# Denominators of a cross-attention through DRAM instead of through a selector product

## What is computed

```
q = shape(query_states @ wq, T);  k = shape(key_value_states @ wk, S);  v = shape(key_value_states @ wv, S)
scores = jnp.einsum('bhtd,bhsd->bhts', q, k) + bias
weights = jax.nn.softmax(scores, axis=-1)
attn = jnp.einsum('bhts,bhsd->bhtd', weights, v)
return transpose(attn) @ wo
x = layernorm(x + cross_attention)
```

## Time and profile before

| | us |
|---|---|
| median of 3 runs | 1098.14 |
| lowest, highest | 1097.65, 1098.8 |
| the profiled execution | 1090.97 |
| its span in the trace | 1089.2 |
| of it: up to the first batch's scores | 154 |
| the 32 batches' scores and what lies between | 154 to 924 |
| projection and feed-forward net | from 932.8 |

### The profile page before, as it was taken

How to read it: one execution, slowest core, us unless ns; L and a number is a source line. 1 busy time by engine, 2 the same in 40 slices (tenths; PEclk the granted TensorE clock), 3 DMA queues, 4 the chain that set the end, 5 groups by cost and what they waited for, 6 DMA issues and landing times. The chain is left out here.

```text
span 1089.2 us, 25588 instructions
## 1 busy us (share of the span) xinstructions
PE 962.5 (88%) x10410; PEld 654.0 (60%) x10410; DVE 717.2 (66%) x1521; ACT 599.0 (55%) x1059; POOL 401.7 (37%) x409
## 2 busy tenths in 40 slices
PE   6474289999999999999999999999999998799996
PEld 4263056666666666666666666666666666545564
DVE  3447277878878777878878777878877874540014
ACT  2132036666666666666666667666666766352232
POOL 7034004555554444555554444555554400000000
PEclk9757579999999999999999999999999999899999
DMA  8664814565556656665555666656555430300000
GB/s 248 163 198 116 170 63 148 171 190 178 164 177 179 191 170 210 181 185 178 163 178 179 191 192 188 186 179 178 164 177 174 141 92 3 109 0 1 1 9 25
DMA packets 57198, 158.16 MB, mean 145 GB/s; under 512 B 23906, under 2 KB 35322, under 8 KB 54010
## 3 DMA queue, kind: packets, MB, share of 16 engines
q1 hardware_dynamic: 57082, 156.54, 48.6%
HBM read 112.40 MB, written 42.63 MB: 142 GB/s over the span
## 5 line engine op out<-in xcount | busy, mean ns | idle before, releaser
L107 DVE TENSOR_REDUCE cmax<-max_ps 112x1 f32<-112x512 f32 x512 | 337.2, 683 | 150.8 <-PE max_ps L97 150.8
L765 ACT ACTIVATE e_sb<-st_ps 128x896 f32<-128x896 f32 (+1 forms) x384 | 354.1, 925 | 149.5 <-DVE st_ps L710 90.4
L97 PE MATMUL max_ps<-kst,qst 111*112 111x512 bf16 x760 | 283.6, 401 | 35.6 <-PEq L116 13.3
L609 PEld LDWEIGHTS st_ps<-qst,kst 114*128 114x128 bf16 (+1 forms) x3072 | 190.6, 101 | 82.0 <-issue 41.9
L811 POOL TENSOR_TENSOR kpart<-k_left,kpart 128x500 bf16<-128x500 f32 x87 | 99.3, 1141 | 344.6 <-ACT k_left L782 340.1
L609 PE MATMUL st_ps<-qst,kst 114*128 114x112 bf16 (+1 forms) x3072 | 214.7, 213 | 12.4 <-DMA qst<-nmp 11.2
L104 DVE CUSTOM_DVE_ANT_0 near_out<-max_ps,near_nat 112x476 bf16<-112x476 f32 x248 | 154.1, 649 | 23.8 <-PE max_ps L97 23.7
L97 PEld LDWEIGHTS max_ps<-kst,qst 111*112 111x112 bf16 x760 | 92.3, 129 | 102.5 <-DVE cmax L107 39.2
L637 PE MATMUL pv_ps<-e_sb,vals 128*32 128x168 f32 (+1 forms) x3072 | 149.4, 312 | 0.3 <-ACT e_sb L765 0.3
L681 PE MATMUL misc<-wv,ctxt 128*128 128x128 f32 (+1 forms) x768 | 107.4, 284 | 6.5 <-DMA ctxt<-in_ctxT 6.5
L681 PEld LDWEIGHTS misc<-wv,ctxt 128*128 128x128 f32 (+1 forms) x768 | 99.5, 193 | 22.3 <-ACT vals L750 11.5
(11 more groups left out here) (124 smaller groups left out, 923.4 us busy)
## 6 DMA issues: line engine op xcount, KB each, us to landing
kst<-kparts SPq DMA_DIRECT2D x192, 375.0 KB, 6.2
kparts<-kpart SPq DMA_DIRECT2D x96, 375.0 KB, 2.7
ctxt<-in_ctxT SPq DMA_DIRECT2D x32, 750.0 KB, 7.1
qst<-qslots SPq DMA_DIRECT2D x192, 28.0 KB, 6.1
qslots<-qst SPq DMA_DIRECT2D x1, 2688.0 KB, 14.5
vals<-in_ctxT SPq DMA_DIRECT2D x3, 750.0 KB, 13.3
h<-in_h SPq DMA_DIRECT2D x2, 1024.0 KB, 7.7
qst<-nmp SPq DMA_DIRECT2D x96, 1.8 KB
```

The costliest lines, as they stand in the source:

```text
L97: return nc.tensor.matmul(dst[0:TT, 0:hi - lo], m.qst[0:M_ROW, r, p, :], m.kst[0:M_ROW, r, p, lo:hi], start=True, stop=True)
L107: return nc.vector.tensor_reduce(m.cmax[:, r, c, p:p + 1], src[0:TT, 0:BOUND[c + 1] - BOUND[c]], AX.X, ALU.max)
L609: mm = nc.tensor.matmul(st_ps[0:K, j % 2, p // 4, (p % 4) * TT:(p % 4 + 1) * TT], m.kst[0:AUG, u % RING, p, j * P:j * P + K], m.qst[0:AUG, ...
L765: nc.scalar.activation(e_sb[0:K, j % E_RING, :].rearrange("p (a c) -> p a c", a=2), st_ps[0:K, j % 2, :, 0:HALF], ACT.Exp).then_inc(s_ex, 1)
```

## The change

The denominators no longer pass through TensorE. Once `x_sb` is there, SyncE stores the four rows of sums into a DRAM buffer `dens` (two DMAs, the second one twice as wide by a broadcast), waits until they are stored, and loads them back spread over the rows (five DMAs) into `den`, as three pieces of 56 columns: one for the twelve heads' groups, two to be added. These stand in SyncE's list between the query pieces and the store of key part 0, with the context load between stores and loads. GpSimd masks `x_sb` itself, adds the pieces (two operations), waits for the loads and adds the two pieces of denominators, all between third 0 and third 1 of the keys. VectorE takes one reciprocal of 112 columns in slot 7 and one product into `m.xh` in slot 9. `sel`, its two products and the copy to `den` are gone.

```
@@ MISC
-        MISC = {0: ("v", 0, 1), 1: ("v", 1, 1), 2: ("v", 2, 1), 3: ("den", 0, -1),
-                4: ("k", 0, 3), 5: ("k", 1, 3), 6: ("k", 2, 3), M0: ("nmt", 0, 1)}
-        NM, REC_A, REC_B, XH = M0 - 1, 4, 5, 9
+        MISC = {0: ("v", 0, 1), 1: ("v", 1, 1), 2: ("v", 2, 1), 4: ("k", 0, 3), 5: ("k", 1, 3), 6: ("k", 2, 3), M0: ("nmt", 0, 1)}
+        NM, REC, XH = M0 - 1, 7, 9
@@ TensorE
-                    if kind == "den":
-                        pe.wait_ge(s_xr, n + 1)
-                        nc.tensor.matmul(misc[:, 0:A_COLS], sel[:, 0, :], x_sb[:, 0:A_COLS], start=True, stop=True)
-                        nc.tensor.matmul(misc[:, A_COLS:A_COLS + B_COLS], sel[:, 1, :],
-                                         x_sb[:, A_COLS:A_COLS + B_COLS], start=True, stop=True).then_inc(s_dn, 1)
@@ VectorE
-                    if j == XH and live(g, u - 1):
-                        dve.wait_ge(s_ro, b)
-                        nc.vector.tensor_tensor(x_own[:, :], x_sb[:, :], rec[:, :], ALU.mult).then_inc(s_xo, 1)
...
-                        if j == REC_A:
-                            dve.wait_ge(s_dr, b)
-                            nc.vector.reciprocal(rec[:, 0:A_COLS], den[:, 0:A_COLS]).then_inc(s_rc, 1)
-                        if j == REC_B:
-                            nc.vector.reciprocal(rec[:, A_COLS:A_COLS + B_COLS],
-                                                 den[:, A_COLS:A_COLS + B_COLS]).then_inc(s_rc, 1)
+                        if j == REC:
+                            dve.wait_ge(s_db, b)
+                            nc.vector.reciprocal(rec[:, :, :], den[:, 0:2, :]).then_inc(s_rc, 1)
                         if j == XH:
-                            dve.wait_ge(s_xo, b)
-                            for i, (lo, hi) in enumerate(((0, A_COLS), (A_COLS, A_COLS + B_COLS))):
-                                nc.vector.tensor_reduce(m.xh[:, i, bass.ds((b - 1) * T, T)],
-                                                        x_own[:, lo:hi].rearrange("p (i t) -> p t i", t=T),
-                                                        AX.X, ALU.add).then_inc(s_xh, 1)
+                            dve.wait_ge(s_rc, b)
+                            dve.wait_ge(s_xs, 2 * b)
+                            nc.vector.tensor_tensor(m.xh[:, :, (b - 1) * T:b * T], x_sum[:, :, :], rec[:, :, :],
+                                                    ALU.mult).then_inc(s_xh, 1)
@@ ScalarE
                         wait(act, s_xo, b - 1)
+                        wait(act, s_ds, 32 * (b - 1))
                         nc.scalar.copy(x_sb[:, :], pv_ps[:, 0:PIECES * T]).then_inc(s_xr, 1)
...
-                        if kind == "den":
-                            act.wait_ge(s_dn, n + 1)
-                            nc.scalar.copy(den[:, :], misc[:, 0:PIECES * T]).then_inc(s_dr, 1)
@@ GpSimd, between split_k(g, u, 0) and split_k(g, u, 1)
-                    pool.wait_ge(s_rc, 2 * b)
-                    nc.gpsimd.tensor_tensor(rec[:, :].rearrange("p (i t) -> p i t", t=T),
-                                            rec[:, :].rearrange("p (i t) -> p i t", t=T),
+                    pool.wait_ge(s_xr, b)
+                    nc.gpsimd.tensor_tensor(x_own[:, :, :], x_sb[:, :].rearrange("p (i t) -> p i t", t=T),
                                             own[:, :].unsqueeze(2).broadcast_to([P, PIECES, T]),
-                                            ALU.mult).then_inc(s_ro, 1)
-                    pool.wait_ge(s_ro, b)
+                                            ALU.mult).then_inc(s_xo, 1)
+                    pool.wait_ge(s_xo, b)
+                    wait(pool, s_xh, b - 1)
+                    nc.gpsimd.tensor_tensor(x_sum[:, :, :], x_own[:, 0:4:3, :], x_own[:, 1:5:3, :],
+                                            ALU.add).then_inc(s_xs, 1)
+                    pool.wait_ge(s_xs, 2 * b - 1)
+                    nc.gpsimd.tensor_tensor(x_sum[:, 0, :], x_sum[:, 0, :], x_own[:, 2, :],
+                                            ALU.add).then_inc(s_xs, 1)
+                    pool.wait_ge(s_dl, 80 * b)
+                    nc.gpsimd.tensor_tensor(den[:, 1, :], den[:, 1, :], den[:, 2, :], ALU.add).then_inc(s_db, 1)
+                    pool.wait_ge(s_db, b)
@@ SyncE, behind stack_k and stack_q
+                if live(g, u - 1):
+                    sp.wait_ge(s_xr, b)
+                    wait(sp, s_dl, 80 * (b - 1))
+                    totals = x_sb[31:P:32, :]
+                    sp.dma_start(m.dens[0, :, :], totals[:, 0:A_COLS + T]).then_inc(s_ds, 16)
+                    sp.dma_start(m.dens[1, :, :].rearrange("q (a c) -> q a c", a=2),
+                                 totals[:, A_COLS:A_COLS + B_COLS].unsqueeze(1).broadcast_to([4, 2, B_COLS])
+                                 ).then_inc(s_ds, 16)
                 if live(g, u + 4):
                     if live(g, u + 1):
                         sp.wait_ge(s_vp, 3 * (b + 2))
                     load_ctx(b + 4, u + 4)
+                if live(g, u - 1):
+                    sp.wait_ge(s_ds, 32 * b)
+                    wait(sp, s_xh, b - 1)
+                    rows = m.dens[0, :, :].rearrange("q (k t) -> (q k) t", t=T).unsqueeze(1)
+                    sp.dma_start(den[:, 0, :], rows.broadcast_to([16, 8, T])).then_inc(s_dl, 16)
+                    for h in range(2):
+                        for i in range(2):
+                            rows = m.dens[1, 2 * i:2 * i + 2, :].rearrange("q (k t) -> (q k) t", t=T).unsqueeze(1)
+                            sp.dma_start(den[64 * h:64 * h + 64, 1 + i, :],
+                                         rows.broadcast_to([8, 8, T])).then_inc(s_dl, 16)
                 if later(g, u + 3):
                     sp.wait_ge(s_kf, 3 * (b + 1))
                     store_k(u + 3, 0)
```

More of the change, by code:

```diff
@@ L500, in cross_attention_block @@
         wk, wv = sb("wk", [C, C]), sb("wv", [C, C])
-        sel = sb("sel", [P, 2, P])
         ctxt = sb("ctxt", [C, RING, S])
@@ L508, in cross_attention_block @@
         nmp, nm_left = sb("nmp", [PAIRS, 3, TT], BF16), sb("nm_left", [PAIRS, TT])
-        x_sb, den, rec = sb("x_sb", [P, PIECES * T]), sb("den", [P, PIECES * T]), sb("rec", [P, PIECES * T])
-        own, x_own = sb("own", [P, PIECES]), sb("x_own", [P, PIECES * T])
+        x_sb, x_own, own = sb("x_sb", [P, PIECES * T]), sb("x_own", [P, PIECES, T]), sb("own", [P, PIECES])
+        x_sum, den, rec = sb("x_sum", [P, 2, T]), sb("den", [P, 3, T]), sb("rec", [P, 2, T])
         max_ps = ctx.enter_context(nc.psum_tensor("max_ps", [P, 2, 512], F32))
@@ L521, in cross_attention_block @@
         s_mx, s_mr = m.s_mx, m.s_mr
-        s_st, s_kp, s_vp, s_nt, s_pv, s_dn = (sem(n) for n in ("st", "kp", "vp", "nt", "pv", "dn"))
-        s_kf, s_ve, s_ex, s_xr, s_nr, s_dr = (sem(n) for n in ("kf", "ve", "ex", "xr", "nr", "dr"))
-        s_kr, s_k3, s_np, s_ro = sem("kr"), sem("k3"), sem("np"), sem("ro")
+        s_st, s_kp, s_vp, s_nt, s_pv = (sem(n) for n in ("st", "kp", "vp", "nt", "pv"))
+        s_kf, s_ve, s_ex, s_xr, s_nr = (sem(n) for n in ("kf", "ve", "ex", "xr", "nr"))
+        s_kr, s_k3, s_np = sem("kr"), sem("k3"), sem("np")
+        s_ds, s_dl, s_xs, s_db = sem("ds"), sem("dl"), sem("xs"), sem("db")
         s_nb, s_nm, s_rc, s_xo, s_xh = (sem(n) for n in ("nb", "nm", "rc", "xo", "xh"))
@@ L596, in misc_free @@
                     else:
-                        pe.wait_ge(s_dr if kind == "den" else s_nr, n + 1)
+                        pe.wait_ge(s_nr, n + 1)
                     return
@@ L669, in iteration @@
                     if isinstance(g, int) and u == -1:
-                        pe.wait_ge(s_w, 16 * 4)
+                        pe.wait_ge(s_w, 16 * 2)
                     misc_free(pe, g, u, j)
@@ L884, in _ @@
                 sp.dma_start(dst[:, :], src).then_inc(s_w, 16)
-            for i in range(2):
-                sp.dma_start(sel[:, i, :], d["sel"][i]).then_inc(s_w, 16)
             for n in range(RING):
@@ L893, in _ @@
             run(iteration)(sp)
-            sp.wait_ge(s_xh, 2 * B)
+            sp.wait_ge(s_xh, B)
 def ffn_block(nc, d, m):
@@ L1124, in build @@
             "(r i c s) -> r i c s", r=RING, i=3, c=C)
+        m.dens = nc.dram_tensor("dens", (2, 4, A_COLS + T), F32, kind="Internal").ap()
         m.s_qd = [ctx.enter_context(nc.semaphore(f"qd{g}")) for g in range(NG)]
```

## The result

| | before | changed |
|---|---|---|
| median of 4 runs, us | 1097.89 | 1238.72 |
| lowest, highest | 1091.1, 1098.8 | 1234.11, 1243.13 |
| profiled execution | 1090.97 | 1239.88 |

The ratio is 1.132, 95% interval 1.128 to 1.135. Keys' loads are 29.47 us apart where they were 24.63.

A forecast was written before the change was run, and what follows sets the result against it. TensorE looked like the bound, each batch closed by GpSimd's chain to `nmp` that just outlasts it. 131 + 6.5 - 1.6 + 4.6 = +140.5 us on the profiled 1091.0, plus 7.1 for the median: 1238 us, range 1165 to 1290.

The forecast's parts named there:

- 28 periods: Batches that load keys: the period grows from 24.63 to 29.3 us, 4.7 us more for 28 batches, +131 us.
- 29th batch: Batch that loads keys but splits none: TensorE is through 24.6 us after the keys' load instead of 18.1, +6.5 us.
- last two batches: Batches with an empty DMA queue: each gains 0.8 us, -1.6 us together.
- `x_sb` to `xh` at the end: End chain with copy, stores, loads, sum, reciprocal and product: 10.1 us instead of 5.5, +4.6 us.
- The loop: Keys' load, stores, denominator loads, third 1, `nmp`, third 2, last key store, next keys' load: 29.3 us, without TensorE.
- rival 1: SyncE's queue: small transfers pass large ones, stores land 2.4 us after issue; period 27.2, +79 us, 1177 us; chance 0.14.
- The mis-sized term: From GpSimd's third 1 to the next keys' load: kept at its old distance of 11.57 us.
- TensorE's fit: TensorE inside the 29.3 us period: stalls near 4 us mid-batch and 1.4 at the end, isn't the bound.
- rival 3: TensorE halts some 4 us a batch and its clock falls; 1 us a batch beyond the stalls, 1266 us; chance 0.08.
- A wait counted twice: TensorE before its first score product waits for `nmp` into `qst`: 20.1 + 11.2 = 31.3 us, 1.0 a batch.
- rival 2: Denominators come in time, only GpSimd's longer list counts: +1.5 - 0.8 = 0.7 a batch, +20 us, 1118 us; chance 0.05.
- rival 4: TensorE's own 95% sets the batch, GpSimd operations and DMAs find room: faster, 1077 us; chance 0.05.

The follow-up runs named there:

- all_late: The changed kernel with GpSimd's four operations behind third 2 and VectorE's reciprocal and product in slots 4 and 5 of the next iteration: 1086.0 us, ratio 0.990.
- pool_ops: The kernel before with three small GpSimd sums (112, 56, 56 columns) into an unread tile behind the mask: 1135.1 us, ratio 1.035.
- late_rec7: all_late with VectorE's reciprocal and product back in slots 7 and 9: 1301.7 us, ratio 1.187.
- act_stores: The changed kernel with the two stores issued by ScalarE on its own queue, right behind its copy to `x_sb`: 1176.8 us, ratio 1.071.

## Why the prediction was right, point by point

| term | predicted, us | measured, us |
|---|---|---|
| 28 periods | +131 | (1008.23 - 183.04) - 689.64 = +135.5 |
| first keys' load, 183.04 for 181.75 | 0 | +1.3 |
| 29th batch, 24.8 for 18.1 | +6.5 | +6.7 |
| last two batches | -1.6 | -1.6 |
| `x_sb` to `xh` at the end, 9.0 for 5.5 | +4.6 | +3.5 |
| projection and feed-forward, 161.7 for 158.2 | 0 | +3.5 |
| sum | 140.5 | 148.9 |

The measured terms are read from these rows: first and last keys' load, the scores after it, and the end chain.

```profile
183.04 0.53 SPq L82 DMA_DIRECT2D kst<-kparts  x1
...
1008.23 1.16 SPq L82 DMA_DIRECT2D kst<-kparts  x2
...
1033.06 0.56 PE L608 MATMUL st_ps<-qst,kst 114*128 114x112 bf16 x8
```

```profile
1068.79 0.39 ACT L758 COPY x_sb<-pv_ps 128x280 f32<-128x280 f32 x1 [1.09 <-PE pv_ps L645]
...
1076.24 0.30 POOL L821 TENSOR_TENSOR den<-den 128x56 f32<-128x56 f32 x1 [5.38 <-DMA den<-dens]
...
1077.47 0.28 DVE L720 TENSOR_TENSOR xh<-x_sum,rec 128x112 f32<-128x112 f32 x1
1078.21 8.99 PE L974 MATMUL ff_ps<-wo_sb,xh 128*112 128x128 f32 x64 [9.49 <-PEq L497]
```

**The median is nearer than the sum deserves.** The terms came out 8.4 us short. What made up for it is the 7.1 us added from the profiled execution of before to its median: in the changed kernel the median lies 1.2 us below the profiled execution. Within the range, but luck.

**The loop, step by step.** The mechanism was as forecast, and its main link was placed well. From keys' load to the first load of `den` it is 12.68 us in the mean; 12.4 was forecast, 10.2 by rival 1. The stores complete 4.7 us after the second's issue, and behind an empty queue in the last batches 1.6 to 1.7: that rejects rival 1. In the trace the completion semaphore of the two stores is raised twice right after their issue and eight times at their landing, so each store waits for four DMA engines alone, which was the ground for rival 1's higher chance; it brought no early landing. Third 1 starts at 17.65 us, forecast 17.7. The parts differ and make up for each other: the first load is 0.3 us later than forecast, the sum on GpSimd takes 0.30 us and was taken at 0.5, the loads land 2.0 us after the last issue and were taken at 2.2. GpSimd idles 3.9 us ahead of the sum and not 2 to 3, mostly because third 0 ends 0.7 us earlier in the mean than in the batch that the prediction read.

**The mis-sized term** is the way back, from third 1 to the next keys' load: 11.81 us in the mean where 11.57 were kept, 6.7 us over 28 batches. Nothing lengthened it. The prediction took it from the one batch at 500.07, and in the kernel before it is 11.2 to 13.4 us, 11.77 in the mean of the 28 batches. It varies with the landing of the last key part, which SyncE waits for. A term that is paid 28 times wants the mean, as the prediction did for the period.

**TensorE's fit.** A halt of near 4 us was forecast and 3.50 is seen; it goes on 18.9 us after the keys' load, forecast 19.2. In this batch the 1.4 us of stall at the end are gone, because TensorE needed 7.1 us (587.27 to 594.36) for what took 5.3; over all batches its wait for `nmp` is 26.2 us, in 25 of them. That is rival 3's mechanism: the clock fell in most batches (23 of 27), and in this one it cost 1.8 us of the 2 us priced, but of stall, not of time. The rival's condition (a loss beyond the stall) was not met where it can be compared: a batch with a halt of 2.10 us and the clock at 1.00 took 28.03 us, one with a halt of 2.15 us and 0.94 took 28.11 (from one copy to `x_sb` to the next).

**A wait counted twice.** The prediction adds 20.1 and 11.2 us to 31.3, 1.0 us a batch. These are the same waits, seen on the weight loads and on the products: in the trace the stretches in which either row stands idle for `nmp` cover 20.2 us. TensorE stood still for 0.65 us a batch. The forecast's sum does not use the figure.

**Ends.** The end chain was over-priced by 1.1 us, with landing times from a busy queue used for an empty one. The 3.5 us behind it were not in the prediction. They have two parts of like size, and the longer halt ahead of the projection (9.49 us instead of 4.69) is neither: the projection takes 8.99 us where it took 8.84. The feed-forward net's first products and the DMA issue ahead of `s`, for which they wait, changed kernel first, then the kernel before:

```profile
1080.62 4.24 SPq L956 DMA_DIRECT2D scales<-in_scales  x4
...
1092.05 5.72 PE L991 MATMUL ff_ps<-x2t,w 128*128 128x448 f32 x10 [4.37 <-DMA s<-in_s]
```

```profile
935.20 2.96 SPq L947 DMA_DIRECT2D scales<-in_scales  x4
...
944.85 4.03 PE L982 MATMUL ff_ps<-x2t,w 128*128 128x448 f32 x10 [2.71 <-DMA s<-in_s]
```

SyncE took 1.3 us longer to issue `scales`, so `s` came later and TensorE waited 4.37 us instead of 2.71. Behind this longer wait the clock fell (it is at 1.00 from 1081.9 to 1092.1 us and at the lower level from there to 1095.5), and the ten products took 5.72 us instead of 4.03. Why the issue took longer stays open.

**Rivals 2 and 4.** Both needed the denominators by 512.6 to 514 in the batch of before, 12.5 to 14 us after the keys' load; they came at 17.2. all_late shows rival 4's ground: with the wait behind everything that the next batch needs, TensorE's work, with VectorE's up to `nmax`, sets the batch. For rival 2's price pool_ops gives a bound: 1.27 us of sums cost 1.2 us a batch with TensorE's two products kept, where the rival had 0.7 for 1.5 us with them gone.

## What to carry to other kernels

A wait in an in-order list costs what stands behind it. The same seven DMAs and the same data cost 141 us with GpSimd's and VectorE's waits ahead of what the next batch needs, 2 us with nobody waiting, and less than nothing with the consumer behind the last thing that the next batch needs. So before a round trip through DRAM is added, close the loop from its issue through the waiting engine back to its issue, add it up once, and compare with the present period. And when an operation is moved later, look at who waits for its buffer to come free: that alone cost 181 us in late_rec7, and one more buffer of 672 bytes a row removed it.

## What the runs showed of the hardware

- A store of 3.5 KB behind eleven loads on the queue takes 4.7 us to complete, 1.6 to 1.7 alone. Issued by ScalarE on its own queue it still takes 5.3 us while a keys' load is under way, and each issue takes 0.50 to 0.53 us of ScalarE.
- The last of five small loads lands 1.9 us after its issue in the changed kernel, and 4.1 in act_stores, where the loads go out 4.2 us sooner after the keys' load.
- In the batch at 568 us a halt of 3.5 us, with TensorE busy for 15.11 of the 16.00 us from 568 to 584, left a granted clock of 0.73 to 0.74 over the 13 us from the halt to the next keys' load; then it was 1.00 again. The clock fell in 23 of 27 batches of the changed kernel.
- A VectorE product of 112 columns takes 0.27 us, and 1.18 when it starts 0.08 us behind a GpSimd operation on 500 columns (1.13 us).
